# Hadamard weight preparation: two-term row sums made by accumulating transfers on GpSimd's queue

## The reference

```
x = fwht(x * SU_ug) / SCALE                                  # over 512
x_up = x @ W_up.T * (Wscale_ug[:INTER] * SCALE)
x_gate = x @ W_gate.T * (Wscale_ug[INTER:] * SCALE)
x = silu(x_gate) * x_up
x = fwht(x * SU_dp) / SCALE                                  # over 2048
x = x @ W_down.T * (Wscale_dp * SCALE)
```

## Time and profile before

| | us |
|---|---|
| median of 3 runs | 2653.99 |
| lowest, highest | 2649.32, 2655.06 |
| the profiled execution | 2655.23 |
| its span, first to last instruction | 2653.4 |

### The profile page before, as it was taken

How to read it: one execution, slowest core, us unless ns; L and a number is a source line. 1 busy time by engine, 2 the same in 40 slices (tenths; PEclk the granted TensorE clock), 3 DMA queues, 4 the chain that set the end, 5 groups by cost and what they waited for, 6 DMA issues and landing times.

```text
span 2653.4 us, 46296 instructions
## 1 busy us (share of the span) xinstructions
PE 2576.0 (97%) x16048; PEld 2187.0 (82%) x16048; DVE 2241.5 (84%) x2573; ACT 1817.0 (68%) x3935; POOL 2044.5 (77%) x1691
## 2 busy tenths in 40 slices
PE   7999989999999999999999999999999999989998
PEld 5566568989888888989888898988888898978888
DVE  6897998899888889898889889898889889889522
ACT  4776777677777777777777767777777777755322
POOL 6776879788787979888797978888797988877222
PEclk9999999999999999999999999999999999989999
DMA  5664246656666665766666665766666666646665
GB/s 181 205 212 167 100 156 208 227 205 234 217 224 227 216 223 198 238 212 227 222 217 224 214 226 197 242 210 236 217 217 221 208 223 214 223 175 230 263 266 186
DMA packets 165209, 564.41 MB, mean 213 GB/s; under 512 B 17264, under 2 KB 19696, under 8 KB 132976
## 3 DMA queue, kind: packets, MB, share of 16 engines
q1 hardware_dynamic: 164976, 561.44, 61.4%
HBM read 527.30 MB, written 34.08 MB: 212 GB/s over the span
## 4 chain that ended last, share of the span: by engine, by line
PE 77%; DVE 11%; ACT 7%; issue 3%; DMA 1%; POOL 0%; SPq 0%; DVEq 0%; ACTq 0%; POOLq 0%
PE pF L726 21%; PE hT L633 14%; PE pM L651 13%; PE pD L742 10%; PE pM L703 8%; DVE h L1180 6%; DVE acc L1193 3%; PE pM L673 3%; PE pD L766 2%; ACT decay L986 2%; PE decay L726 2%; PE hT L625 1%; PE pF L766 1%; ACT delta L963 1%; ACT delta L958 1%
## 5 line engine op out<-in xcount | busy, mean ns | idle before, releaser
L1180 DVE TENSOR_TENSOR_SCAN h<-decay,dbx 128x512 f32<-128x512 f32 x1024 | 1201.2, 1206 | 92.8 <-ACT decay L986 64.4
L1362 POOL TENSOR_TENSOR dbx<-u,bb 128x2048 f32<-128x2048 f32 (+1 forms) x272 | 1179.2, 4336 | 37.6 <-DVE h L1180 35.6
L986 ACT ACTIVATE decay<-delta,a_neg 128x255 f32<-128x255 f32 x2048 | 875.9, 468 | 315.5 <-DVE h L1180 308.7
L1193 DVE SCALAR_TENSOR_TENSOR acc<-hT,bcT,acc 128x1024 f32<-128x1024 f32 x480 | 610.0, 1271 | 122.5 <-PE hT L633 118.9
L726 PE MATMUL pF<-fxT_hi,wug 128*128 128x256 f32 x3632 | 709.9, 288 | 0.4 <-issue 0.4
L633 PEld LDWEIGHTS hT<-ident,h 128*128 128x128 f32 x4096 | 472.9, 141 | 144.2 <-issue 88.4
L726 PEld LDWEIGHTS pF<-fxT_hi,wug 128*128 128x128 f32 x3632 | 582.9, 192 | 0.9 <-issue 0.9
L633 PE MATMUL hT<-ident,h 128*128 128x128 f32 x4096 | 535.8, 274 | 36.1 <-DVE acc L1193 24.9
L726 PE MATMUL pF<-fxT_lo,wug 128*128 128x256 f32 x1816 | 514.3, 283 | 0.0
L651 PE MATMUL pM<-xnT,w_in 128*128 128x256 f32 x2016 | 480.4, 382 | 3.4 <-ACT hid L906 1.9
L651 PEld LDWEIGHTS pM<-xnT,w_in 128*128 128x128 f32 x2016 | 367.7, 192 | 51.1 <-issue 5.0
(11 more groups left out here) (173 smaller groups left out, 2719.6 us busy)
## 6 DMA issues: line engine op xcount, KB each, us to landing
wug<-scratch_ug SPq DMA_DIRECT2D x243, 1024.0 KB, 4.8
wd<-scratch_wd SPq DMA_DIRECT2D x243, 512.0 KB, 4.1
w_in<-in_W_in SPq DMA_DIRECT2D x252, 256.0 KB, 2.9
bb<-scratch_bc SPq DMA_DIRECT2D x128, 256.0 KB, 4.6
xb<-in_hidden_states SPq DMA_DIRECT2D x16, 512.0 KB, 5.2
xr<-in_hidden_states SPq DMA_DIRECT2D x16, 512.0 KB, 5.8
out<-xr SPq DMA_DIRECT2D x15, 512.0 KB, 3.6
kept_ug<-scratch_ug SPq DMA_DIRECT2D x7, 1024.0 KB, 8.2
```

What stands on the lines that cost most here:

```text
L986: e = act.activation(da[q % 2][:, i, 1:], delta[c % 2][:, dt, 1:], ACT.Exp, scale=a_neg[:, dt, n:n + 1])
L1180: dve.tensor_tensor_scan(row(h[n % 2][:, tiles, :]), row(da[q % 2][:, :, :]), row(dbx[n % 2][:, tiles, :]), 0.0, ALU.mult, ALU.add).then_i ...
L1193: dve.scalar_tensor_tensor(acc[c % 2][:, tb, :], hT[:, :], cn, acc[c % 2][:, tb, :], ALU.mult, ALU.add).then_inc(acc_done, 1)
L1362: pool.tensor_tensor(dbx[n % 2][:, tiles, :], u[:, tiles, :], rows, ALU.mult).then_inc(done if restarts(c) else prod_done, 1)
```

## The change

The six last groups of up and gate (SUMMED) no longer take four products per output tile. Their input buffer has six tiles, three pairs of two-term sums of row tiles: (0+2, 1+3), (1+2, 0+3) and (0+1, 2+3). With W0 to W3 for the row tiles, each of the four rows of the 4x4 transform is the sum or difference of the two members of one pair. The first terms are plain loads on SP, four transfers of 256 or 512 KB. The second terms are three transfers of 512 KB issued by GpSimd with accumulation, so that the transfer adds into what lies in SBUF. GpSimd waits for all first terms (had_part) before it issues them, TensorE waits for the sums (had_summed) before the group's first product. Groups up 0 and up 1 (WHOLE) stay as they were, with one input buffer, and all down groups now come before up 1. Two sum buffers alternate.

The plan of the slots changes too. Up to slot 19 of chunk 0 the room is 4 in slots 0 and 10 to 13, else 2. From slot 20 on (FIRST_SUM), counted through both chunks, groups of 8 products take four slots of room 2, then two slots have none (EACH = 6); the last such group ends in slot 21 of chunk 1, where before the last product stood in slot 28. The set r is stored one slot earlier. add_rows stands at the end of GpSimd's even slot, some five or six slots after the last product of the buffer's last user.

```diff
-        had_in1 = first("had_in1", [P, KT, DM])
-        had_in2 = first("had_in2", [P, KT, DM])
-    had_in = (had_in0, had_in1, had_in2)
+        had_sum1 = first("had_sum1", [P, KT + 2, DM])
+        had_sum0 = first("had_sum0", [P, 2, DM])
+    sum_tiles = ((had_in0[:, 0:2, :], had_in0[:, 2:4, :], had_sum0[:, :, :]),
+                 (had_sum1[:, 0:2, :], had_sum1[:, 2:4, :], had_sum1[:, 4:6, :]))
...
-        GROUPS = ([("up", 0), ("down", 0), ("up", 1)] + [("down", q) for q in range(1, KT)] + [("up", q) for q in range(2, KT)]
-                  + [("gate", q) for q in range(KT)])
+        GROUPS = ([("up", 0)] + [("down", q) for q in range(KT)] + [("up", q) for q in range(1, KT)] + [("gate", q) for q in range(KT)])
...
+        WHOLE, SUMMED = UG_GROUPS[:2], UG_GROUPS[2:]
+        SUM_BUF = {g: (i + 1) % 2 for i, g in enumerate(SUMMED)}
+        SUM_USE = {g: i // 2 for i, g in enumerate(SUMMED)}
+        LAST_USER = dict(zip(SUMMED, [LAST_DOWN, WHOLE[1]] + SUMMED))
+        FIRSTS, SECONDS = (slice(0, 2), (1, 0), slice(0, 4, 2)), (slice(2, 4), slice(2, 4), slice(1, 4, 2))
...
-        steps_of = lambda o: 2 if GROUPS[o // KT][0] == "down" else KT
+        steps_of = lambda o: KT if o // KT in WHOLE else 2
...
+        FIRST_SUM, EACH = 20, 6
...
-                room = (4 if k == 0 or 8 <= k < 16 else 3 if 23 <= k < 28 else 2) if c == 0 else 2
+                at = SLOTS * c + k
+                room = (4 if k == 0 or 10 <= k < 14 else 2) if at < FIRST_SUM else 2 * ((at - FIRST_SUM) % EACH < KT)
...
-                            HAD_STORE[divmod(SLOTS * c + k + 2, SLOTS)].append(o // KT)
-                            HAD_LOAD[at] += UG_GROUPS[3:5] if o // KT == LAST_DOWN else next_in(o // KT) if o // KT in UG_GROUPS else []
+                            HAD_STORE[divmod(at + (1 if SETS[g] == "r" else 2), SLOTS)].append(g)
+                            for new in [i for i in SUMMED if LAST_USER[i] == g]:
+                                HAD_LOAD[divmod(at + 1, SLOTS)].append(new)
+                                HAD_ADD[divmod((at + 6) // 2 * 2, SLOTS)].append(new)
...
             def load_had(g):
...
+                wait_first(sp, had_mm, KT * (LAST_USER[g] + 1), sp_passed)
+                for dst, rows in zip(sum_tiles[SUM_BUF[g]], FIRSTS):
+                    if isinstance(rows, slice):
+                        sp.dma_start(dst, had_rows(g)[:, rows, :]).then_inc(had_part[SUM_BUF[g]], 16)
+                    else:
+                        for a, row in enumerate(rows):
+                            sp.dma_start(dst[:, a, :], had_rows(g)[:, row, :]).then_inc(had_part[SUM_BUF[g]], 16)
...
+                    if g in SUMMED and r == 0:
+                        pe.wait_ge(had_summed[SUM_BUF[g]], 16 * len(SECONDS) * (SUM_USE[g] + 1))
...
+                elif g in SUMMED:
+                    pair, last, minus = (0, 0, 2, 1)[r], i == 1, i * (r > 0)
+                    src = sum_tiles[SUM_BUF[g]][pair][:, i if r < 3 else 1 - i, :]
...
+            def add_rows(g):
+                pool.wait_ge(had_part[SUM_BUF[g]], 16 * 4 * (SUM_USE[g] + 1))
+                for dst, rows in zip(sum_tiles[SUM_BUF[g]], SECONDS):
+                    pool.dma_start(dst, had_rows(g)[:, rows, :], accum_op=ALU.add).then_inc(had_summed[SUM_BUF[g]], 16)
...
+                for g in HAD_ADD.get((c, k), ()):
+                    add_rows(g)
```

More of the change, by code:

```diff
@@ L166, in fused_block @@
         w_out_in = sem("w_out_in"); down_in = [sem("down_in0"), sem("down_in1")]; wscale_in = sem("wscale_in")
-        had_loaded = [sem(f"had_loaded{i}") for i in range(len(had_in))]
+        had_loaded = sem("had_loaded"); had_part = [sem("had_part0"), sem("had_part1")]; had_summed = [sem("had_summed0"), sem("had_summed1")]
         had_setup = sem("had_setup"); w_first_in = sem("w_first_in"); diag_done = sem("diag_done"); turned_dve = sem("turned_dve"); turned_pool = sem("turned_pool")
@@ L315, in split_row, with had_rows @@
             return t[:, r, :].rearrange("p (a m) -> p a m", a=KT) if GROUPS[g][0] == "down" else t[:, :, :].rearrange("p a (k m) -> p k a m", k=KT)[:, r, :, :]
+        def had_rows(g):
+            name, q = GROUPS[g]
+            return W[f"W_{name}"].rearrange("(k p) f -> p k f", p=P)[:, :, DM * q:DM * (q + 1)]
         def bank_tiles(o):
@@ L322, in had_scale @@
             return row_scale[:, KT * GROUPS[g][1] + r:KT * GROUPS[g][1] + r + 1] if GROUPS[g][0] == "down" else su_ug[:, r:r + 1]
-        HAD_PE, HAD_EVAC, HAD_STORE, HAD_LOAD = ({(c, k): [] for c in range(2) for k in range(SLOTS)} for i in range(4))
-        steps_of = lambda o: 2 if GROUPS[o // KT][0] == "down" else KT
+        HAD_PE, HAD_EVAC, HAD_STORE, HAD_LOAD, HAD_ADD = ({(c, k): [] for c in range(2) for k in range(SLOTS)} for i in range(5))
+        steps_of = lambda o: KT if o // KT in WHOLE else 2
         HAD_EVAC[0, 0] += [3]
         HAD_STORE[0, 1] += [0]
-        HAD_LOAD[0, 0] += UG_GROUPS[1:2]
+        HAD_LOAD[0, 0] += WHOLE[1:]
+        FIRST_SUM, EACH = 20, 6
         todo = [(o, i) for o in range(KT, NTILE) for i in range(steps_of(o))]
@@ L331, in fused_block @@
             for k in range(SLOTS):
-                room = (4 if k == 0 or 8 <= k < 16 else 3 if 23 <= k < 28 else 2) if c == 0 else 2
+                at = SLOTS * c + k
+                room = (4 if k == 0 or 10 <= k < 14 else 2) if at < FIRST_SUM else 2 * ((at - FIRST_SUM) % EACH < KT)
                 while room and todo:
                     o, i = todo.pop(0)
+                    g = o // KT
                     HAD_PE[c, k].append((o, i))
@@ L337, in fused_block @@
                     if i == steps_of(o) - 1:
-                        at = divmod(SLOTS * c + k + 1, SLOTS)
-                        HAD_EVAC[at].append(o)
+                        HAD_EVAC[divmod(at + 1, SLOTS)].append(o)
                         if o % KT == KT - 1:
-                            HAD_STORE[divmod(SLOTS * c + k + 2, SLOTS)].append(o // KT)
-                            HAD_LOAD[at] += UG_GROUPS[3:5] if o // KT == LAST_DOWN else next_in(o // KT) if o // KT in UG_GROUPS else []
+                            HAD_STORE[divmod(at + (1 if SETS[g] == "r" else 2), SLOTS)].append(g)
+                            for new in [i for i in SUMMED if LAST_USER[i] == g]:
+                                HAD_LOAD[divmod(at + 1, SLOTS)].append(new)
+                                HAD_ADD[divmod((at + 6) // 2 * 2, SLOTS)].append(new)
         DVE_COLS = 400
@@ L470, in load_had @@
                 name, q = GROUPS[g]
[L471 to L475, removed]
+                if g in WHOLE:
+                    if g:
+                        wait_first(sp, had_mm, KT * (WHOLE[0] + 1), sp_passed)
+                    sp.dma_start(had_in0[:, :, :], had_rows(g)).then_inc(had_loaded, 16)
+                    return
+                wait_first(sp, had_mm, KT * (LAST_USER[g] + 1), sp_passed)
[5 more added lines that the diff above has]
+                            sp.dma_start(dst[:, a, :], had_rows(g)[:, row, :]).then_inc(had_part[SUM_BUF[g]], 16)
             def store_had(g):
@@ L758, in had @@
                         pe.wait_ge(had_lo, o - len(had_bank) + 1)
[L759 to L762, removed]
+                    if g in WHOLE and r == 0:
+                        pe.wait_ge(had_loaded, 16 * (WHOLE.index(g) + 1))
+                    if g in SUMMED and r == 0:
+                        pe.wait_ge(had_summed[SUM_BUF[g]], 16 * len(SECONDS) * (SUM_USE[g] + 1))
+                if g in WHOLE:
+                    src, last, minus = had_in0[:, i, :], i == KT - 1, (r & i).bit_count() % 2
+                elif g in SUMMED:
+                    pair, last, minus = (0, 0, 2, 1)[r], i == 1, i * (r > 0)
+                    src = sum_tiles[SUM_BUF[g]][pair][:, i if r < 3 else 1 - i, :]
                 else:
```

## The result

| | us |
|---|---|
| before, median of 4 runs | 2654.45 |
| after, median of 4 runs | 2737.84 (2735.91 to 2740.78) |
| ratio, 95% interval | 1.0321 (1.0309 to 1.0334) |
| forecast | 2645, range 2636 to 2661 |

The account below looks back on a forecast made before the run. No plain TensorE bound: TensorE was close to full in A, C, D and G, VectorE in B and nearly in G. The stretches' terms summed to -11.6 us, with +2.0 for traffic -9.6, hence 2645, range 2636 to 2661.

Parts of the forecast that it names:

- GpSimd's issues: 18 accumulating transfers in GpSimd's program, three per group: 1.2 us each, 3.6 us per group, hidden behind group 1.
- dear issues: Rival: at 3 us or more per issue, taps and silu come late; G +6, C +3, 2654; 10 in 100.
- C: Chunk 0, slots 18 to 23: one more evacuation and perhaps a wait for the first sum; +1.7 us (0 to +7).
- G: Chunk 1, slots 10 to 17: TensorE loses work, but VectorE and GpSimd stay full; 0 us (-1 to +6).
- TensorE's wait for the sums: TensorE before the summed groups' first products: a sum takes 12 to 13 us; 1 us at group 1, none later.
- Late sums: Slower rival: accumulating transfers run well below plain ones; 2656 at 20 us per sum, 2666 at 25; 13 in 100.
- D: Chunk 0, slots 24 to 31: fewer products, the 4.6 us of waits for turns go; -4.6 us (-5.3 to -1).
- B: Chunk 0, slots 10 to 17: VectorE is full and five evacuations go elsewhere; -3.0 us (-3.3 to -1).
- F: Chunk 1, slots 4 to 9: the 5.3 us wait for the had_r_lo store goes; -3.6 us (-4.6 to 0).
- A: Chunk 0, slots 0 to 9: four products fewer, three more evacuations mostly hidden; -0.6 us (-1.8 to +2.0).
- H: Chunk 1, slots 18 to 31: two evacuations fewer, some loss to TensorE's lower clock; -0.8 us (-1.8 to +2).
- GpSimd starved: Rival: each issue first waits out a VectorE operation, 1.2 us on each of three issues; 2652 us, 5 in 100.

Follow-up runs that it names:

- e4_free_pe: Changed kernel, but TensorE's products of summed groups read columns of w_dt and don't wait for the sums; 2703.6 us (one run).
- e1_ring: Changed kernel with GpSimd's descriptor area raised from 1024 to 3072 bytes per partition, b_out's tile left out; 2682.0 us, ratio 1.0112 to the kernel before.
- e3_no_add: Changed kernel without GpSimd's 18 accumulating transfers, TensorE waiting for the first terms only; 2648.0 us, ratio 0.998 to the kernel before.
- e8b_store: Kernel before with only the stores of set r one slot earlier; 2650.3 us, ratio 0.9992.
- e2_plain: Changed kernel with its 18 GpSimd transfers as plain loads instead of accumulating ones; 2653.0 us (one run; before 2653.4).

## Why the prediction was wrong

**The step that failed first: "GpSimd's issues", 1.2 us each, 3.6 per group.** The record of one is indeed 1.2 us. But I bounded the engine's stop above by "the whole landing of a 512 KB load, 4.1 us", and a held issue stops the engine for 5 to 10 us more, 12.9 to 18.0 per group. What was missing is that an issue can be held until the transfer before it has ended, and that the size of the descriptor area decides this. The rival "dear issues" had the right chain behind the issue, but no hold in it, and the wrong price: 3 us per issue where it was 5, and only in C and G, so 2654 where the hold alone made 2704 (e4_free_pe).

**The step that failed second: "TensorE's wait for the sums".** I counted 12.0 us to "the first product of slot 20", 16 for group 2 and "four slots or more" for the others. The slots were never laid out one by one. I took FIRST_SUM as the place where summed groups begin, but `room` says only how many products a slot takes. Slot 19 had room and nothing else to do. That one slot moved all six groups, and cost 28 us. As to the landing, 12 to 13 us was nearly right for issues that stand back to back: some 14 in e1_ring. In after it is 23 us at the first group, as the holds come on top. "Late sums" was the rival that named this wait; it decided "at some 19 us from GpSimd's first issue", but by its leads of 12 and 16 us it came to 2666 at the most.

**The wait that I costed at nothing.** "Cover gone, each us of issue would cost one" held: GpSimd's product behind the first issues was late by 16.6 us (170.22 for 153.57), and VectorE stood for 13.9. In G the spare time of GpSimd was smallest, and G lost most but D.

**What was right.** Without the accumulating transfers the sum stands at -7.9 in e3_no_add's stretches, against my -11.6, and with the +2.0 for traffic at -9.6 to -5.3 measured in the medians. By terms: B -3.7 for -3.0. D -2.6 for -4.6: I had all 4.6 us of waits for turns gone, and part came back elsewhere. F -2.4 for -3.6, where e8b_store has -3.0 for the store alone. C +1.0 for +1.7, 1.0 of which was for late sums. G +1.5 for 0. A +2.2 for -0.6: I had the evacuations hidden, but VectorE is busy 39.68 of 45.08 there, 1.9 more than before (that these 1.9 are the 2.2 is argued, no run parts them). H -2.9 for -0.8. The products' records are fewer by 96 (320 and 224), as forecast, B and C were 35.3 and 26.6 us long, and no wait for had_r_lo stood in F; but VectorE was idle 4.7 us in D, not 2 or less. My signs of failure were TensorE standing over 3 us at slots 20 or 26, and issues over 2 us each: the first came true (16.87 and 18.26 us, at slots 19 and 23), the second only with the idle time before the record counted in.

**The landing, the port and the room.** From the issue's record to the landing one transfer took 5.4 us at the least and 6.2 in the median. By the Trainium skill ("DMA: Bandwidth & Descriptors", on the anatomy of a GpSimd-issued DMA) it would be 2.0 us and 1.2 for the bytes, an estimate of 3.2. The trace doesn't agree: none of after's accumulating transfers was under 5.4. My own 12 to 13 us for three stands against some 14; what was missed was the hold more than the landing. e2_plain's three issues took 2.38 us while VectorE did a scan and an add into acc, so "GpSimd starved" is out. The condition in the Trainium skill ("SBUF — State Buffer", the box on DVE blocking such a DMA), an operation like a copy on VectorE, wasn't met, and the trace agrees. One sentence that I hadn't weighed bears on the hold: the Trainium skill ("Perfetto Trace Analysis", section "DMA Instruction — SWDGE (GPSIMD)") says that a DMA engine may start before all descriptors are written, "particularly if more descriptors are generated than fit in the descriptor buffer". By that the room can run out; that GpSimd then stands, and at what price, is shown by after against e1_ring.

## What to carry to other kernels

A transfer issued by an engine that computes is priced by how long that engine may be held, not by the record of its issue: space such transfers so that each has landed before the next, or give their descriptors room. Before a wait is placed by slots, lay out the plan slot by slot as the code would, above all where an "if" leaves a slot with room and nothing else to fill it. And when the gain is bounded by a few us (here 5) and the new waits are not, price the waits first.

## What the runs showed of the hardware

- An accumulating transfer of 512 KB made 256 packets of 2 KB and 16 of 4 bytes, a plain one from the same queue 128 of 4 KB and 16 of 4 bytes. They took 178 ns per 2 KB and 159 ns per 4 KB, 2.2 times the time per byte; SP's queue took 84 ns per 2 KB. In after the packets of one such transfer took 3.2 to 5.6 us. Three that were issued in a row (e1_ring) ran nearly one after the other, 10 to 12 us in all. The Trainium skill ("Collectives: The Full Stack", section "The bandwidth ceiling: the fold count and why AG ≠ RS ≠ AR") says of the adding DMA in collectives that it takes two source descriptors per chunk. Twice the time per byte would fit that; no run here shows the reads themselves, and the greater count of packets comes from their size alone.
- With 1024 bytes a partition for descriptors only one accumulating transfer was under way, with 2048 or 3072 three were, while three plain ones were issued in a row with 1024.
- A wait of TensorE costs more than its length: the products after 16.87 us of idling ran at a granted clock of 0.50, 3.75 us instead of 1.88 for two.
- GpSimd's records behind an accumulating issue are longer without costing more: the copy of the carry 0.68 us for 0.19 in after, and behind three issues in a row (e1_ring) 1.68, the product after it 6.01 for 4.55. From start to start that product took 4.7 us (155.48 to 160.15), so the records overlap what follows them.
